# A fused attention and feed-forward kernel: the cast of x moved from ScalarE to GpSimd, and new orders on four engines

## The chip, the core and the metric
The kernel runs on one core of a Trainium2 chip. The metric is the device time of one execution in microseconds (us). The engines are TensorE (PE; its weight loads are PEld), VectorE (DVE), ScalarE (ACT), GpSimd (POOL) and SyncE (SP), which here only issues DMAs. Each engine runs its own list of instructions in order; semaphores tie the lists together.

## The reference
x has the shape (16, 128, 32, 32): 16 batches of 1024 tokens with 128 channels. What is computed, cut to what matters:

```
x  = einsum('oc,bchw->bohw', inv(I - circulant(ricker(width, damp))), x)
t  = tokens(x)                                  # (16, 1024, 128)
t1 = t + attention(layernorm(t))                # causal linear attention, 8 heads of 16,
                                                # features elu(.) + 1, running sums of K V and of K
z  = layernorm(t1)
g  = mean over tokens of (relu(z gfc1' + b) gfc2' + b)
W1m = W1 + sum_e g_e tv_W1[e]     W2m = W2 + sum_e g_e tv_W2[e]      # weights of each batch
out = t1 + layernorm(z + W2m relu(W1m z + b1m) + b2m) * gain + bias
```

## The kernel before
The first phase (some 20 to 490 us) goes over 128 tiles of 128 tokens, eight to a batch, and makes t1, z and the sums of the gate. The second phase is the feed-forward part. The diff touches only the first phase.

Nearly every product is made from float16 parts: a tensor is split into a high part (its float16 cast) and a low part (the rest, again cast), and three products are added. For x the parts are x_hi and x_lo, two tiles (128x256) to an instruction.

What sets the order is written out by hand. Each engine has a table such as SCALAR_ORDER: names of stages, each with a skew. In slot s the engine runs, for each name in the table's order, that stage for tile s - skew. One pass over the eight slots of a batch is `batch`; `run` unrolls the first two batches, loops over the middle ones and unrolls the rest. An engine whose next instruction waits on a semaphore holds up all that stands behind it.

The stages that the change and the prediction speak of:
- split_x stands in two tables. On ScalarE (L722) it makes x_hi; on GpSimd (L1036) it makes x_lo when x_hi is ready. Both act in even slots, for tiles s and s + 1. x_hi has room for eight tiles, so the cast waits (`wo_done`) until out_project has read the tiles eight back.
- conv (L559) and project (L571) multiply x by the inverse and by the weights of q, k and v. stats1 and mean_var1 take the layernorm's variance from conv's result, and rsqrt (L977, GpSimd) makes the factor, for both layernorms at once.
- exp_qk, relu_qk, v_hi (ScalarE), make_qk and v_lo (VectorE) form q, k and v. qk_hi and qk_lo (GpSimd) split q and k, and SyncE's turn (L467) transposes the parts by DMA (qkT_parts).
- scores (L606), scores_hi and scores_lo make the causal products in p_a; values (L629) multiplies by v and adds the state of earlier tiles; denominator, invert and divide finish the attention; turn_out, copy_out and out_project (L660) bring it back and add conv's product a second time, from the same x_hi and x_lo.
- read_t1, stats2, mean_var2, shift2, normalise, z_hi, z_lo (GpSimd) and SyncE's turn_z make z and its transposed parts; gate and gate_relu use them.
- tv_hi and tv_lo (L844, VectorE) split the expert weights, a quarter of a share of each batch at a time; they serve the second phase.

The lists of instructions are in PSUM's and SBUF's terms double or fourfold buffered: p_in has two banks, p_a one set, qkT_parts and z_parts four places.

Of the kernel before, what the change touches and what calls it, by code (L numbers as in the profile page):

```python
# [11 lines left out]
ACT = mybir.ActivationFunctionType  # L12
AX = mybir.AxisListType

B, C, T = 16, 128, 1024
P = 128
TILES = T // P
NT = B * TILES
HALF = 4
# [19 lines left out]

TENSOR_ORDER = [("state", 3), ("scores", 4), ("conv", 0), ("turn_out", 6), ("values", 5), ("out_project", 6),
                ("gate", 13), ("project", 0)]
SCALAR_ORDER = [("normalise", 10), ("split_x", 0), ("relu_qk", 2), ("read_t1", 7), ("gate_relu", 14),
                ("exp_qk", 1), ("state_hi", 3), ("v_hi", 1), ("tv_hi", 0), ("scores_hi_0", 4), ("copy_out", 6),
                ("scores_hi_1", 4)]
VECTOR_ORDER = [("shift2", 9), ("divide", 6), ("make_qk", 2), ("v_lo", 2), ("stats2", 7), ("stats1", 0),
                ("state_lo", 3), ("mean_var1", 0), ("mean_var2", 7), ("scores_lo_0", 4), ("denominator", 5),
                ("scores_lo_1", 4), ("tv_lo", 1), ("invert", 5)]
GPSIMD_ORDER = [("rsqrt", 1), ("z_hi", 10), ("split_x", 0), ("z_lo", 10), ("qk_hi", 2), ("qk_lo", 2),  # L50
                ("last_rsqrt2", 8)]
SYNC_ORDER = [("turn_z", 10), ("turn", 2), ("load_x", 3), ("load_tv", 3), ("store", 8)]

# [76 lines left out]
def build(nc, d):  # L130

    top = ExitStack()
    with top:
# [61 lines left out]
        x_loaded = [sem(f"x_loaded_{i}") for i in range(2)]  # L195
        ones_set = sem("ones_set")
# [12 lines left out]
        xh_ready, xl_ready = sem("xh_ready"), sem("xl_ready")  # L209
# [172 lines left out]
        with early, ExitStack() as pa_:  # L382
# [41 lines left out]
            def at_least(eng, s, value):  # L424

                if not isinstance(value, int) or value > 0:
                    eng.wait_ge(s, value)

            def batch(stages, b, behind=None):

                for slot in range(TILES):
                    for k, stage_ in stages:
                        d, t = divmod(slot - k, TILES)
                        if isinstance(b, int) and not 0 <= b + d < B:
                            continue
                        stage_(b + d, t)
                    if behind:
                        behind(TILES * (b - B) + slot)

            def run(eng, order, stages, behind=None):  # L440
                stages = [(skew, stages[name]) for name, skew in order]
                for b in range(2):
                    batch(stages, b)
                with eng.Fori(2, B) as b:
                    batch(stages, b)
                for b in range(B, B + 2):
                    batch(stages, b, behind)

            MEAN, VAR, RSTD, SHIFT = 9, 10, 11, 12
            PAIRED = 7  # L450
# [4 lines left out]
            with nc.Block() as block:  # L455
# [263 lines left out]

                @block.scalar  # L720
                def _(act):
                    def split_x(b, t):  # L722
                        if t % 2 or isinstance(b, int) and TILES * b + t == 0:
                            return
                        n = TILES * b + t
                        hf, j = t // HALF, t % HALF
                        if j == 0:
                            act.wait_ge(x_loaded[hf], 16 * (b + 1))
                        at_least(act, wo_done, n - TILES + 2)
                        cols = slice(j * P, (j + 2) * P)  # L730
                        nc.scalar.activation(xh[:, hf, cols], xf[:, hf, cols], ACT.Copy).then_inc(xh_ready, 1)

                    def tv_hi(b, t):
                        if t % 2:
                            return
# [79 lines left out]
                    def merged_w1_hi(slot):  # L815
# [6 lines left out]
                                             p_in[:, k % 2, :].rearrange("p (j m) -> p m j", j=4), ACT.Copy)\  # L822
                            .then_inc(mhi_ready, 1)

                    run(act, SCALAR_ORDER, {"tv_hi": tv_hi, "split_x": split_x, "read_t1": read_t1, "v_hi": v_hi,
                        "exp_qk": exp_qk, "relu_qk": relu_qk,
                        "scores_hi_0": scores_hi(0), "scores_hi_1": scores_hi(1),
                        "copy_out": copy_out, "normalise": normalise, "state_hi": state_hi, "gate_relu": gate_relu}, merged_w1_hi)
# [144 lines left out]
                @block.gpsimd  # L973
                def _(pool):
                    mhalf = kcol("mhalf")

                    def rsqrt(b, t):  # L977
                        n = TILES * b + t
                        both = not isinstance(n, int) or n >= PAIRED
                        pool.wait_ge(mv1, n + 1)  # L980
                        if both:
                            pool.wait_ge(mv2, n - PAIRED + 1)
                        s = sts[:, 0:2 if both else 1, t % 4, :]
                        nc.gpsimd.tensor_tensor(s[:, :, RSTD], s[:, :, VAR], mhalf[:, 0:2 if both else 1], ALU.pow)\  # L984
                            .then_inc(rstd, 1)

                    def last_rsqrt2(b, t):
                        n = TILES * b + t
                        if not isinstance(n, int) or n < NT - PAIRED:
                            return  # L990
                        s = st2[:, (t + 3) % 4, :]
                        pool.wait_ge(mv2, n + 1)
                        nc.gpsimd.tensor_tensor(s[:, RSTD:RSTD + 1], s[:, VAR:VAR + 1], mhalf[:, 0:1], ALU.pow)\
                            .then_inc(rstd, 1)

                    def parts_at(t, q_at, k_at, dims):

                        tile = pk[:, t % 4, :, :, :].rearrange("p w h c -> p (w h c)")
                        return bass.AP(tile.tensor, tile.offset + q_at,
                                       [list(tile.ap[0]), [NH * 4 * DH + k_at - q_at, 2], [4 * DH, NH], *dims])  # L1000

                    def qk_hi(b, t):
                        n = TILES * b + t
                        made, used = (n + 1, n - 3) if isinstance(n, int) else (pool.to_reg(n + 1), pool.to_reg(n - 3))
                        pool.wait_ge(ones_set, 1)
                        pool.wait_ge(qk_ready, made)
                        for i in range(2):
                            at_least(pool, sc_done[i], used)
                        src = qk[:, t % 4, :].rearrange("p (w h i) -> p w h i", h=NH, i=DH)
                        nc.gpsimd.tensor_copy(parts_at(t, 0, DH, [[DH, 2], [1, DH]]),  # L1010
                                              src.unsqueeze(3).broadcast_to([P, 2, NH, 2, DH])).then_inc(hi_ready, 1)

                    def qk_lo(b, t):
                        n = TILES * b + t
                        pool.wait_ge(hi_ready, n + 1)
                        nc.gpsimd.tensor_tensor(parts_at(t, 2 * DH, 0, [[1, DH]]),  # L1016
                                                qk[:, t % 4, :].rearrange("p (w h i) -> p w h i", h=NH, i=DH),
                                                pk[:, t % 4, :, :, DH:2 * DH], ALU.subtract).then_inc(lo_ready, 1)

                    def z_hi(b, t):  # L1020
                        n = TILES * b + t
                        made, used = n + 1, 32 * b + 16 * (t // 4)
                        if not isinstance(n, int):
                            made, used = pool.to_reg(made), pool.to_reg(used)
                        pool.wait_ge(ones_set, 1)
                        pool.wait_ge(z_ready, made)
                        at_least(pool, z_turned[t % 4], used)
                        nc.gpsimd.tensor_copy(zp[:, t % 4, 0, :], z_[:, t % 2, :]).then_inc(zhi_ready, 1)

                    def z_lo(b, t):  # L1030
                        n = TILES * b + t
                        pool.wait_ge(zhi_ready, n + 1)
                        nc.gpsimd.tensor_tensor(zp[:, t % 4, 1, :], z_[:, t % 2, :], zp[:, t % 4, 0, :], ALU.subtract)\
                            .then_inc(zlo_ready, 1)

                    def split_x(b, t):  # L1036
                        if t % 2 or isinstance(b, int) and TILES * b + t == 0:
                            return
                        hf, j = t // HALF, t % HALF
                        cols = slice(j * P, (j + 2) * P)  # L1040
                        pool.wait_ge(xh_ready, TILES // 2 * b + t // 2 + 1)
                        nc.gpsimd.tensor_tensor(xl[:, hf, cols], xf[:, hf, cols], xh[:, hf, cols], ALU.subtract)\
                            .then_inc(xl_ready, 1)

                    run(pool, GPSIMD_ORDER, {"rsqrt": rsqrt, "qk_lo": qk_lo,
                        "split_x": split_x,
                        "last_rsqrt2": last_rsqrt2, "qk_hi": qk_hi, "z_hi": z_hi, "z_lo": z_lo})


        with ExitStack() as pb:  # L1050
# [428 lines left out]
```

## Time and profile before

| | us |
|---|---|
| median of 3 runs | 747.9 (747.24 to 750.97) |
| profiled execution | 749.55 |
| its span, first to last instruction | 747.8 |

| engine | busy us | share of the span | instructions |
|---|---|---|---|
| PE | 692.5 | 93% | 12002 |
| PEld | 533.8 | 71% | 12002 |
| DVE | 659.1 | 88% | 2409 |
| ACT | 649.1 | 87% | 1780 |
| POOL | 465.2 | 62% | 790 |

The mean clock granted to TensorE is 0.975 of full speed. In the slices of the page PE, DVE and ACT stand at 90% or more through the steady part of the first phase, POOL at 80% or more; after about 470 us DVE, ACT and above all POOL have less to do. The time that SyncE takes to issue a DMA isn't counted as busy in this table; it is seen in the timeline of its queue (SPq). A duration is that of one instruction from its start to its end, and consecutive instructions of an engine may overlap by some tens of nanoseconds, so start to start is often less.

### The profile page before, as it was taken

The numbers are of one execution on the slowest core, as the hardware profiler recorded it, in microseconds if no ns is written. First come the engines' busy times: TensorE is split into PE (matmuls) and PEld (weight loads), VectorE is DVE, ScalarE is ACT, GpSimd is POOL, SyncE is SP. The second block draws the span as 40 slices with busy tenths as digits, with TensorE's granted clock in tenths as the row PEclk, the third lists the DMA queues.
The fourth block names the chain that finished last, engine by engine and source line by source line (L and its number), as shares of the span: only waits on it lengthen the run. The fifth ranks groups of instructions, "written<-read, shape, count | busy, mean of one in ns | idle before, by whom it ended". The sixth has DMA issues, their size and how long they took to land. (4 is left out here: it accounts for less than half of the span.)

```text
span 747.8 us, 38168 instructions
## 1 busy us (share of the span) xinstructions
PE 692.5 (93%) x12002; PEld 533.8 (71%) x12002; DVE 659.1 (88%) x2409; ACT 649.1 (87%) x1780; POOL 465.2 (62%) x790
## 2 busy tenths in 40 slices
PE   4898899999999999999999999888999998999993
PEld 2576677777777777777777777775777787777772
DVE  5697889999999999999999999768898977998983
ACT  4797989999999999999999999557888876888883
POOL 3686778888888888888888888421333321333333
PEclk9798999999999999999999999899999999999998
DMA  4757676666666666666666666410222211222221
GB/s 149 112 110 134 132 129 129 148 143 131 148 142 132 148 141 132 148 141 134 148 139 135 148 142 123 74 51 1 73 85 83 71 58 31 85 70 84 84 84 70
DMA packets 202485, 82.66 MB, mean 111 GB/s; under 512 B 176093, under 2 KB 189824, under 8 KB 202377
## 3 DMA queue, kind: packets, MB, share of 16 engines
q1 hardware_dynamic: 202440, 82.08, 48.3%
q8 instruction: 26, 0.43, 0.2%
q14 instruction: 19, 0.15, 0.1%
HBM read 22.79 MB, written 17.30 MB: 54 GB/s over the span
## 5 line engine op out<-in xcount | busy, mean ns | idle before, releaser
L892 DVE SCALAR_TENSOR_TENSOR scores_lo<-p_a,scores_hi 128x512 f16<-128x512 f32 x256 | 173.3, 683 | 1.7 <-ACT scores_hi L786 1.3
L786 ACT ACTIVATE scores_hi<-p_a 128x512 f16<-128x512 f32 x256 | 156.2, 611 | 9.3 <-PE p_a L623 9.3
L1010 POOL CAST qk_parts<-qk_f 128x512 f16<-128x512 f32 x128 | 78.0, 610 | 50.2 <-issue 24.9
L1442 POOL TENSOR_TENSOR ffn_rstd_shift<-ffn_rstd_shift,consts 128x4 f32<-128x4 f32 x32 | 36.5, 1142 | 109.1 <-DVE ffn_rstd_shift L1400 109.1
L984 POOL TENSOR_TENSOR stats<-stats,consts 128x2 f32<-128x2 f32 (+1 forms) x128 | 88.2, 689 | 17.9 <-DVE stats L925 13.1
L1224 PE MATMUL psb<-merged_W_of_batch,h_hi 128*128 128x128 f16 x512 | 94.5, 220 | 2.2 <-DVE h_lo L1378 1.5
L1378 DVE TENSOR_TENSOR h_lo<-h_f,h_hi 128x512 f16<-128x512 f32 x128 | 95.6, 786 | 1.1 <-ACT h_hi L1280 1.1
L1269 ACT ACTIVATE h_f<-psb,merged_b_of_batch 128x512 f32<-128x512 f32 x128 | 87.2, 709 | 10.3 <-PE psb L1205 8.6
L1225 PE MATMUL psb<-merged_W_of_batch,h_hi 128*128 128x128 f16 x512 | 94.2, 220 | 0.0
L1226 PE MATMUL psb<-merged_W_of_batch,h_lo 128*128 128x128 f16 x512 | 94.1, 220 | 0.0
L1016 POOL TENSOR_TENSOR qk_parts<-qk_f,qk_parts 128x256 f16<-128x256 f32 x128 | 85.9, 671 | 10.2
L640 PE MATMUL p_o<-v_parts,scores_hi 128*128 128x17 f16 x1024 | 90.3, 171 | 1.8 <-issue 0.2
L640 PEld LDWEIGHTS p_o<-v_parts,scores_hi 128*128 128x128 f16 x1024 | 82.1, 96 | 12.4 <-issue 11.7
L644 PE MATMUL p_o<-v_parts,scores_lo 128*128 128x17 f16 x1024 | 89.8, 171 | 0.0
L642 PE MATMUL p_o<-v_parts,scores_hi 128*128 128x16 f16 x1024 | 89.6, 170 | 0.0
L642 PEld LDWEIGHTS p_o<-v_parts,scores_hi 128*128 128x128 f16 x1024 | 80.5, 96 | 1.0
L644 PEld LDWEIGHTS p_o<-v_parts,scores_lo 128*128 128x128 f16 x1024 | 80.1, 96 | 0.0
L1435 POOL TENSOR_TENSOR normed<-normed,ln_gain_rows 128x512 f32<-128x512 f32 x32 | 40.6, 1268 | 59.5 <-ACT normed L1289 59.5
L1289 ACT ACTIVATE normed<-psb,ffn_rstd_shift 128x128 f32<-128x128 f32 x128 | 48.1, 456 | 33.8 <-DVE ffn_rstd_shift L1406 33.8
L801 ACT ACTIVATE z<-t,stats 128x128 f32<-128x128 f32 x128 | 65.5, 512 | 0.9 <-DVE stats L875 0.9
L765 ACT ACTIVATE exp_qk<-p_in,stats 128x256 f32<-128x256 f32 x128 | 60.8, 475 | 3.7 <-POOL stats L984 2.1
L616 PE MATMUL p_a<-mask_factors_bf 64*128 64x256 bf16 x512 | 60.2, 277 | 3.5 <-DVE scores_lo L892 1.2
(215 smaller groups left out, 2697.5 us busy)
## 6 DMA issues: line engine op xcount, KB each, us to landing
x_f<-in_x SPq DMA_DIRECT2D x32, 256.0 KB, 3.2
t_rows<-t SPq DMA_DIRECT2D x64, 128.0 KB, 1.8
t_back<-t_rows SPq DMA_DIRECT2D x32, 256.0 KB, 2.6
out<-out_tile SPq DMA_DIRECT2D x32, 256.0 KB, 2.1
tv_share<-in_L_ffn_tv_W SPq DMA_DIRECT2D x32, 128.0 KB, 2.2
qkT_parts<-qk_parts SPq DMA_TRANSPOSE x128, 3.1
zT_hi_lo<-z_parts SPq DMA_TRANSPOSE x128, 2.3
merged_W<-in_L_ffn_W SPq DMA_DIRECT2D x2, 256.0 KB, 4.4
```

The source lines that it names most:

```text
L640: mm(num[:, h, :], hi, vp[:, t, h, 0:VW], start=(h == 0), stop=False, skip_group_check=True)
L642: mm(num[:, h, 0:DH], hi, vp[:, t, h, VW:VW + DH], start=False, stop=False, skip_group_check=True)
L644: last = mm(num[:, h, :], lo, vp[:, t, h, 0:VW], start=False, stop=True, skip_group_check=True)
L786: nc.scalar.activation(ah[:, t % 2, cols], p_a[:, cols], ACT.Relu).then_inc(ahi_ready[eo], 1)
L892: nc.vector.scalar_tensor_tensor(al[:, t % 2, cols], p_a[:, cols], 0.0, ah[:, t % 2, cols], ALU.max, ALU.subtract).then_inc(alo_ready[eo], 1)
L984: nc.gpsimd.tensor_tensor(s[:, :, RSTD], s[:, :, VAR], mhalf[:, 0:2 if both else 1], ALU.pow)\
L1016: nc.gpsimd.tensor_tensor(parts_at(t, 2 * DH, 0, [[1, DH]]), qk[:, t % 4, :].rearrange("p (w h i) -> p w h i", h=NH, i=DH), pk[:, t % 4, : ...
L1224: mm(o, hi, w2b[:, bb, 0, c, :], start=False, stop=False)
L1225: mm(o, hi, w2b[:, bb, 1, c, :], start=False, stop=False)
L1226: last = mm(o, lo, w2b[:, bb, 0, c, :], start=False, stop=(c == FC - 1))
L1269: nc.scalar.activation(hf_[:, c, :], ps[:, c, :], ACT.Relu, bias=b1s[:, h // 2, c:c + 1], scale=1.0 / WS).then_inc(h_ready[c], 1)
L1378: nc.vector.tensor_tensor(hl[:, h % 2, c, :], hf_[:, c, :], hh[:, h % 2, c, :], ALU.subtract)\
```

## The change
ScalarE's split_x goes. GpSimd gets it as x_hi with skew -1: in odd slots, as the last stage, for the two tiles of the next slot; the old split_x of GpSimd is now x_lo and stands right behind rsqrt. tv_lo of VectorE moves from behind the scores_lo pair to behind mean_var1. Stages change places in the tables of TensorE, ScalarE and VectorE; SYNC_ORDER stays. GpSimd's loop ends one batch earlier (`upto`), since the last batch has no next tiles to cast.

```diff
-TENSOR_ORDER = [("state", 3), ("scores", 4), ("conv", 0), ("turn_out", 6), ("values", 5), ("out_project", 6),
-                ("gate", 13), ("project", 0)]
+TENSOR_ORDER = [("state", 3), ("scores", 4), ("turn_out", 6), ("conv", 0), ("values", 5), ("gate", 13),
+                ("out_project", 6), ("project", 0)]
...
-GPSIMD_ORDER = [("rsqrt", 1), ("z_hi", 10), ("split_x", 0), ("z_lo", 10), ("qk_hi", 2), ("qk_lo", 2),
+GPSIMD_ORDER = [("rsqrt", 1), ("x_lo", 0), ("z_hi", 10), ("z_lo", 10), ("qk_hi", 2), ("qk_lo", 2), ("x_hi", -1),
...
-            def run(eng, order, stages, behind=None):
+            def run(eng, order, stages, behind=None, upto=B):
...
-                with eng.Fori(2, B) as b:
+                with eng.Fori(2, upto) as b:
                     batch(stages, b)
-                for b in range(B, B + 2):
-                    batch(stages, b, behind)
+                for b in range(upto, B + 2):
+                    batch(stages, b, behind if b >= B else None)
...
-                    def split_x(b, t):
-                        if t % 2 or isinstance(b, int) and TILES * b + t == 0:
-                            return
-                        n = TILES * b + t
-                        hf, j = t // HALF, t % HALF
-                        if j == 0:
-                            act.wait_ge(x_loaded[hf], 16 * (b + 1))
-                        at_least(act, wo_done, n - TILES + 2)
-                        cols = slice(j * P, (j + 2) * P)
-                        nc.scalar.activation(xh[:, hf, cols], xf[:, hf, cols], ACT.Copy).then_inc(xh_ready, 1)
...
+                    def x_hi(b, t):
+                        if t % 2 or isinstance(b, int) and TILES * b + t == 0:
+                            return
+                        n = TILES * b + t
+                        hf, j = t // HALF, t % HALF
+                        loaded, used = 16 * (b + 1), n - TILES + 2
+                        if not isinstance(n, int):
+                            loaded, used = pool.to_reg(loaded), pool.to_reg(used)
+                        pool.wait_ge(ones_set, 1)
+                        if j == 0:
+                            pool.wait_ge(x_loaded[hf], loaded)
+                        at_least(pool, wo_done, used)
+                        cols = slice(j * P, (j + 2) * P)
+                        nc.gpsimd.tensor_copy(xh[:, hf, cols], xf[:, hf, cols]).then_inc(xh_ready, 1)
+
+                    def x_lo(b, t):
```

On GpSimd, at the border of an odd slot and the even one behind it, in the loop, the list was this. qk_f, qk_parts are q and k and their parts, stats holds the factors of rsqrt, x_f, x_hi and x_lo are x and its parts, z_parts those of z:

```order
L1004 REGISTER_ALU
L1010 CAST qk_parts<-qk_f 128x2x8x32 [waits sc_done_0,sc_done_1,qk_ready,ones_set]
L1016 TENSOR_TENSOR qk_parts<-qk_f,qk_parts 128x2x8x16 [waits hi_ready]
L980 REGISTER_ALU
L982 REGISTER_ALU [waits mv1]
L984 TENSOR_TENSOR stats<-stats,consts 128x2 [waits mv2]
L1024 REGISTER_ALU
L1028 CAST z_parts<-z 128x128 [waits z_turned_0,z_ready,ones_set]
L1041 REGISTER_ALU
L1042 TENSOR_TENSOR x_lo<-x_f,x_hi 128x256 [waits xh_ready]
```

Now, with the code's lines a little earlier, the same place reads:

```order
L998 CAST qk_parts<-qk_f 128x2x8x32 [waits sc_done_0,sc_done_1,qk_ready,ones_set]
L1004 TENSOR_TENSOR qk_parts<-qk_f,qk_parts 128x2x8x16 [waits hi_ready]
L1031 ISA
L1037 CAST x_hi<-x_f 128x256 [waits wo_done,ones_set]
L968 REGISTER_ALU
L970 REGISTER_ALU [waits mv1]
L972 TENSOR_TENSOR stats<-stats,consts 128x2 [waits mv2]
L1044 REGISTER_ALU
L1045 TENSOR_TENSOR x_lo<-x_f,x_hi 128x256 [waits xh_ready]
L1012 REGISTER_ALU
```

The cast x_hi has come in between qk_lo and rsqrt, with its wait on out_project (wo_done), and x_lo has moved up from behind z_hi to behind rsqrt.

On VectorE, in an odd slot of the loop, from the two variances (BN_AGGR; the one that waits on bn1 is mean_var1, on bn2 mean_var2) to invert (RECIPROCAL), the list was this:

```order
L842 BN_AGGR stats<-stats 128x2 [waits bn1,ones_set]
L925 BN_AGGR stats<-stats 128x2 [waits bn2,ones_set]
L890 REGISTER_ALU [waits av_done]
L892 SCALAR_TENSOR_TENSOR scores_lo<-p_a,scores_hi 128x512 [waits ahi_ready_0]
L899 TENSOR_SCALAR denominators<-p_o 128x8 [waits av_done]
L892 SCALAR_TENSOR_TENSOR scores_lo<-p_a,scores_hi 128x512 [waits ahi_ready_1,av_done]
L848 ISA
L850 ISA [waits tv_hi_ready]
L850 SCALAR_TENSOR_TENSOR tv_lo<-tv_share,tv_hi 128x128
L905 RECIPROCAL denominators<-denominators 128x8 [waits den1]
```

Now, from state_lo (state_parts) on:

```order
L871 TENSOR_TENSOR state_parts<-p_s,state_parts 128x136 [waits sh_ready]
L830 BN_AGGR stats<-stats 128x2 [waits bn1,ones_set]
L836 ISA
L838 ISA [waits tv_hi_ready]
L838 SCALAR_TENSOR_TENSOR tv_lo<-tv_share,tv_hi 128x128
L878 REGISTER_ALU [waits av_done]
L880 SCALAR_TENSOR_TENSOR scores_lo<-p_a,scores_hi 128x512 [waits ahi_ready_0]
L887 TENSOR_SCALAR denominators<-p_o 128x8 [waits av_done]
L880 SCALAR_TENSOR_TENSOR scores_lo<-p_a,scores_hi 128x512 [waits ahi_ready_1,av_done]
L893 RECIPROCAL denominators<-denominators 128x8 [waits den1]
```

tv_lo stood between the second scores_lo and invert; now it stands between mean_var1 and the first scores_lo, and mean_var2 has gone further ahead.

## Rows read from the trace of the kernel before

**Rows 1.** Busy time of each engine, 130 to 450 us: window, its length, then PE, PEld, DVE, ACT, POOL
```profile
130.00:450.00 320.00, 307.54 (x6468) 237.42 (x6468) 309.46 (x1228) 317.42 (x999) 270.84 (x505) 1.00 0.65 141
```

**Rows 2.** Waits of SyncE's queue, 73 to 456 us: total us, times, longest us
```profile
SPq L427 <- POOL qk_parts L1016: 1.3, 4, 0.7
```

**Rows 3.** Timeline of SyncE's queue, one batch: start us, duration us, instruction
```profile
297.36 1.23 SPq L473 DMA_TRANSPOSE qkT_parts<-qk_parts  x1
...
300.37 1.18 SPq L482 DMA_TRANSPOSE zT_hi_lo<-z_parts  x1
...
303.94 1.17 SPq L482 DMA_TRANSPOSE zT_hi_lo<-z_parts  x1
305.31 1.23 SPq L473 DMA_TRANSPOSE qkT_parts<-qk_parts  x1
...
308.83 1.23 SPq L473 DMA_TRANSPOSE qkT_parts<-qk_parts  x1
...
325.33 1.23 SPq L473 DMA_TRANSPOSE qkT_parts<-qk_parts  x1
```

**Rows 4.** The tile qk_parts, 130 to 450 us: ns min/median/max, and landing
```profile
L473 SPq DMA_TRANSPOSE qkT_parts<-qk_parts x92: 1231/1232/1382, 129.3 to 448.2; - x92
...
DMA to landing us min/median/max: 3.0/3.1/3.3
```

**Rows 5.** Timeline of GpSimd around the even slot of tile 82
```profile
303.99 0.70 POOL L984 TENSOR_TENSOR stats<-stats,consts 128x2 f32<-128x2 f32 x1
304.64 0.29 POOL L1028 CAST z_parts<-z 128x128 f16<-128x128 f32 x1
304.89 0.79 POOL L1042 TENSOR_TENSOR x_lo<-x_f,x_hi 128x256 f16<-128x256 f32 x1
...
306.04 0.61 POOL L1010 CAST qk_parts<-qk_f 128x512 f16<-128x512 f32 x1
306.73 0.68 POOL L1016 TENSOR_TENSOR qk_parts<-qk_f,qk_parts 128x256 f16<-128x256 f32 x1
...
309.83 0.67 POOL L1016 TENSOR_TENSOR qk_parts<-qk_f,qk_parts 128x256 f16<-128x256 f32 x1
```

**Rows 6.** Timeline of ScalarE (first row) and TensorE, same stretch
```profile
304.33 0.42 ACT L731 ACTIVATE x_hi<-x_f 128x256 f16<-128x256 f32 x1
...
303.86 0.44 PE L669 MATMUL p_m<-w_outT,attn_outT 128*128 128x128 f32 x2
...
305.91 0.23 PE L567 MATMUL p_m<-w_in_hi,x_hi 128*128 128x128 f16 x1 [0.22 <-POOL x_lo L1042]
...
306.09 0.28 PE L658 MATMUL p_m<-consts,attn_out 128*128 128x128 f32 x1
306.38 0.17 PE L640 MATMUL p_o<-v_parts,scores_hi 128*128 128x17 f16 x1
...
310.70 0.44 PE L669 MATMUL p_m<-w_outT,attn_outT 128*128 128x128 f32 x2
...
312.15 0.39 PE L623 MATMUL p_a<-qkT_parts 64*128 64x128 f16 x8
```

**Rows 7.** Timeline of VectorE (L850, L842) and GpSimd (L1042), two slots
```profile
304.87 0.28 DVE L850 SCALAR_TENSOR_TENSOR tv_lo<-tv_share,tv_hi 128x128 f32 x1
...
310.23 0.18 DVE L842 BATCH_NORM_AGGREGATE stats<-stats 128x2 f32<-128x9 f32 x1
...
318.59 0.67 POOL L1042 TENSOR_TENSOR x_lo<-x_f,x_hi 128x256 f16<-128x256 f32 x1
318.73 0.67 DVE L850 SCALAR_TENSOR_TENSOR tv_lo<-tv_share,tv_hi 128x128 f32 x1
```

**Rows 8.** Waits of SyncE's queue, 20 to 73 us, then 456 to 500 us
```profile
SPq L427 <- POOL qk_parts L1016: 9.2, 5, 3.1
SPq L471 <- POOL qk_parts L1016: 4.1, 4, 2.8
...
SPq L481 <- POOL z_parts L1033: 8.7, 6, 2.4
```

More of the change, by code:

```diff
@@ L38 @@
 BIG = -1.0e30
-TENSOR_ORDER = [("state", 3), ("scores", 4), ("conv", 0), ("turn_out", 6), ("values", 5), ("out_project", 6),
-                ("gate", 13), ("project", 0)]
[L44 to L49, printed above, removed]
-GPSIMD_ORDER = [("rsqrt", 1), ("z_hi", 10), ("split_x", 0), ("z_lo", 10), ("qk_hi", 2), ("qk_lo", 2),
+TENSOR_ORDER = [("state", 3), ("scores", 4), ("turn_out", 6), ("conv", 0), ("values", 5), ("gate", 13),
+                ("out_project", 6), ("project", 0)]
+SCALAR_ORDER = [("relu_qk", 2), ("normalise", 10), ("read_t1", 7), ("gate_relu", 14), ("state_hi", 3),
+                ("tv_hi", 0), ("exp_qk", 1), ("v_hi", 1), ("copy_out", 6), ("scores_hi_0", 4), ("scores_hi_1", 4)]
+VECTOR_ORDER = [("shift2", 9), ("divide", 6), ("stats2", 7), ("make_qk", 2), ("mean_var2", 7), ("v_lo", 2),
+                ("stats1", 0), ("state_lo", 3), ("mean_var1", 0), ("tv_lo", 1), ("scores_lo_0", 4),
+                ("denominator", 5), ("scores_lo_1", 4), ("invert", 5)]
+GPSIMD_ORDER = [("rsqrt", 1), ("x_lo", 0), ("z_hi", 10), ("z_lo", 10), ("qk_hi", 2), ("qk_lo", 2), ("x_hi", -1),
                 ("last_rsqrt2", 8)]
@@ L823, in merged_w1_hi @@
                             .then_inc(mhi_ready, 1)
-                    run(act, SCALAR_ORDER, {"tv_hi": tv_hi, "split_x": split_x, "read_t1": read_t1, "v_hi": v_hi,
+                    run(act, SCALAR_ORDER, {"tv_hi": tv_hi, "read_t1": read_t1, "v_hi": v_hi,
                         "exp_qk": exp_qk, "relu_qk": relu_qk,
@@ L1034, in z_lo @@
                             .then_inc(zlo_ready, 1)
-                    def split_x(b, t):
+                    def x_hi(b, t):
[13 more added lines that the diff above has]
+                    def x_lo(b, t):
                         if t % 2 or isinstance(b, int) and TILES * b + t == 0:
@@ L1045, in _ @@
                     run(pool, GPSIMD_ORDER, {"rsqrt": rsqrt, "qk_lo": qk_lo,
-                        "split_x": split_x,
-                        "last_rsqrt2": last_rsqrt2, "qk_hi": qk_hi, "z_hi": z_hi, "z_lo": z_lo})
+                        "x_hi": x_hi, "x_lo": x_lo,
+                        "last_rsqrt2": last_rsqrt2, "qk_hi": qk_hi, "z_hi": z_hi, "z_lo": z_lo}, upto=B - 1)
         with ExitStack() as pb:
```

## The prediction, made before the result was known

> **What bounds the kernel now.** I read the busy shares first, then the waits, then the order of time of one queue. In the long steady stretch of the first phase ScalarE is busy for 317 of 320 us, VectorE for 309 and TensorE for 308 [rows 1], so ScalarE looks like the bound, and the change takes work from it. The waits say otherwise. The queue that issues the DMAs (SyncE) waits 1.3 us in all between 73 and 456 us, four times [rows 2]: of 383 us it stands idle for a third of a per cent. Its timeline is one issue behind another, 1.2 us for each transpose, two transposes a tile [rows 3, 4]. From the transpose of q and k at 297.36 to the same one a batch later at 325.33 it takes 27.97 us for eight tiles [rows 3]. The queue is late, not early: the parts of tile 80 are finished at 306.73 + 0.68 = 307.41 [rows 5], their transpose is issued at 308.83 [rows 3], lands 3.1 us later [rows 4] at about 311.93, and TensorE takes it up at 312.15 [rows 6]. So finished work waits for the queue, and the reader of the result comes just behind the landing. Neither side has time to give away.
>
> A second cycle is as long. A pair of tiles of x can be cast only when out_project has read the pair whose place it takes. In [rows 6] out_project ends at 303.86 + 0.44 = 304.30 (call this O). The cast starts on ScalarE at 304.33 and takes 0.42, x_lo on GpSimd runs from 304.89 to 305.68 [rows 5], and conv starts at 305.91, after an idle 0.22 that ends with x_lo [rows 6]. O to conv is 1.61. From conv to the end of out_project two slots on (310.70 + 0.44 = 311.14) TensorE takes 5.23. Together that is 6.84 for this pair of tiles, against 27.97 / 4 = 6.99 for the queue. Four such pairs make a batch, and the other pairs are as near. So the steady stretch, 383 / 27.97 = 13.7 batches, has two bounds of nearly one length.
>
> **The change part by part.**
> SyncE: its program is unchanged, instruction for instruction, so 27.97 us a batch is a floor that the change does not touch. Nothing gained elsewhere shortens the steady stretch.
>
> ScalarE: 63 casts of 0.42 go. They lie beside the queue's floor; worth 0.
>
> GpSimd: 63 casts of 128x256 come. No such cast stands in the trace. The casts beside it are z_hi with 128 columns, 0.29, and qk_hi with 512, 0.61 [rows 5]; these are my bounds, and the straight line between them gives 0.40. GpSimd is busy for 271 of 320 us [rows 1]; 46 casts of 0.40 are 18.4, which makes 289, or 90%: it fits, but with little room.
>
> The wait for out_project moves with the cast. On ScalarE it was the second stage of the even slot; now it stands last in the odd slot of GpSimd, and behind it are queued rsqrt, then x_lo. That the cast is a slot ahead in the program doesn't make it earlier: out_project of the pair seven tiles back ends at O in either case. The new path from O to conv: the wake, 0.14 (as from the cast's end at 304.75 to x_lo at 304.89; below, the 0.03 of ScalarE); the cast, 0.40 (0.29 to 0.61); rsqrt, 0.65 from start to start, 303.99 to 304.64 (0.70 by its duration) [rows 5]; x_lo, 0.67 undisturbed [rows 7] (0.79 in [rows 5]); conv, 0.23 as now. The sum is 2.09, between 1.85 and 2.47, where it was 1.61.
>
> TensorE: turn_out goes ahead of conv. It held up the products with v by 0.29 (306.09 to 306.38) [rows 6]; ahead of conv it falls into time in which conv waits for x_lo. Conv to O is then 5.23 - 0.29 = 4.94. The gate's change of place with out_project adds nothing: both lie between the same conv and the same later out_project.
>
> VectorE: tv_lo leaves its place ahead of invert. It takes 0.28 when it starts before x_lo, and 0.67 when x_lo is 0.14 ahead [rows 7]; then invert, divide and turn_out come late. I take the pair without this delay (the 5.23 above) for all four, so this gain is in the sum. In its new place tv_lo stands ahead of both scores_lo. On GpSimd qk_lo runs from 309.83 to 310.50 [rows 5] where mean_var1 ends at 310.41 [rows 7], so it will still meet an operation there and may be held by 0.67 - 0.28 = 0.39. Behind it wait scores_lo and then the next scores on TensorE. That stretch of TensorE has the 0.22 in which it idles now, plus 2.09 - 1.61 = 0.48, less 0.29 for turn_out, or 0.41. The hold is just covered: 0, and if the cover goes 0.1 a pair costs 5.5 us in all (4 x 13.7 pairs).
>
> The Trainium skill, SBUF — State Buffer (Who interferes with whom), says that a VectorE instruction with two inputs in SBUF and a GpSimd instruction that reads SBUF exclude each other, and that the one that starts first holds the other up. The trace agrees: 0.28 or 0.67 by which of the two was first. By that rule the new place, too, costs a hold in each pair; what that would make is the third rival.
>
> ScalarE's other stages and the rest of VectorE's order change their places beside the floor; with no row that shows a wait of theirs, 0. The stretches outside the floor, where SyncE waits for its data (9.2 and 4.1 us before 73 us, 8.7 after 456 [rows 8]), may move either way: 0, with 5 us on both sides.
>
> Sum: a pair takes 2.09 + 4.94 = 7.03, a batch 28.12, 0.15 over the queue's 27.97; 13.7 batches make +2.1 us. The profiled execution took 749.55 (its span 747.8 and 1.75 around it), so it would take 751.6; the median shown is 1.65 lower, and the forecast is **750.0**. Not a gain, because the queue's floor stays, and hardly a loss, because the new chain is about as long as the floor.
>
> **The rivals.**
> First, GpSimd's chain decides and the kernel is slower. It decides from 27.97 / 4 - 4.94 = 2.05 us between O and conv; each 0.1 above is 5.5 us. With the cast at 0.51, half way to the row of 512 columns, the chain is 2.20, and the time 747.9 + 0.15 x 54.8 = 756; at 2.47 it is 771. For it: every step is in one queue behind one wait, and the forecast lies only 0.04 above the point. Against it: the row nearest to the cast in kind is z_hi, the shorter one.
>
> Second, the steady stretch stays, and its ends get shorter: ScalarE loses 0.42 in each pair and tv_lo its 0.39 in some; in some six pairs of the first batches and of the last that is up to 5 us, 743. For it: SyncE waits there for GpSimd's parts. Against it: GpSimd gets the cast there too.
>
> Third, the hold on tv_lo isn't covered. At 0.2 a pair it costs 0.2 x 54.8 = 11, so 759. For it: qk_lo and mean_var1 end within 0.1 us of each other. Against it: the spare 0.41 on TensorE. It decides as soon as the hold is over 0.41.
>
> Fourth, ScalarE really is the bound: 63 x 0.42 = 26 us would go, 722. Against it speaks the queue without waits; I see no way around that.
>
> **How the numbers follow.** Forecast 0.48, first rival 0.32, second 0.09, third 0.08, fourth 0.03. Half a per cent, 3.7 us, is about what can be told from no change. Faster by more: second and fourth, 0.12. Slower by more: first and third, 0.40. Same: 0.48. The forecast's own range is 746 to 752. The range for 8 in 10 leaves out the fourth rival, a part of the second, and the upper end of the first and third: 744.5 to 759.5.
>
> **What would show it.** In the changed profile: SyncE again almost without waits between 73 and 456 us, and a batch of 27.97 there, if the floor holds; if a batch is longer, waits of SyncE for qk_parts appear. ScalarE's busy share falls by about 6% and shows idle time. x_hi on GpSimd starts 0.1 to 0.2 behind the end of out_project and takes 0.40; rsqrt starts at once behind it; conv of every even slot waits for x_lo, some 2.1 behind O. No invert waits behind a long tv_lo. The forecast is wrong if SyncE's batch gets shorter than 27.9 us (its issues then weren't a floor), or if x_hi starts well before O or runs for over 0.5.

## The result, and the profile after

The changed kernel takes 762.57 us (median of 4 runs, 760.76 to 764.65), the kernel before 748.91 on the same chip (747.24 to 750.97): a ratio of 1.018, with a 95% interval of 1.015 to 1.021. It is slower by 13.7 us; the forecast was 750.0, with a range up to 759.5. The profiled execution has a span of 759.0 us against 747.8.

The loss lies in the steady stretch of the first phase. The view of one tile gives a measure of a batch that works for every kernel here: x_lo runs four times a batch, and the row gives its number and its first and last start between 130 and 450 us. Before, then after (nanoseconds min/median/max, first to last start in us):

```profile
L1042 POOL TENSOR_TENSOR x_lo<-x_f,x_hi x46: 668/722/795, 130.1 to 444.5; 128x256 f16<-128x256 f32 x46
```
```profile
L1045 POOL TENSOR_TENSOR x_lo<-x_f,x_hi x45: 669/672/677, 130.3 to 448.0; 128x256 f16<-128x256 f32 x45
```
(444.5 - 130.1) / 45 x 4 is 27.95 us a batch before; (448.0 - 130.3) / 44 x 4 is 28.88 after. The 0.93 times 13.7 batches is 12.7 us: the whole loss, within the spread of single runs (13.7 by the medians, 11.2 by the two profiled spans). All batches given below are worked out in this way.

Busy time of the engines after, 130 to 450 us, answers to [rows 1], and the waits of SyncE's queue, 73 to 456 us, to [rows 2]:

```profile
130.00:450.00 320.00, 304.48 (x6246) 234.62 (x6247) 294.76 (x1189) 301.05 (x920) 275.14 (x533) 1.00 0.63 137
```
```profile
SPq L480 <- POOL z_parts L1021: 11.4, 46, 0.5
```
ScalarE went from 317 to 301 us, and no engine is as busy as before: this is a kernel that waits. SyncE, which had waited 1.3 us in all, waits 11.4 us for z_parts, so its queue is a bound no longer. Who waits instead is in the waits of the engines, same stretch (us in total, times, longest):

```profile
POOL x_hi L1037 <- PE p_m L668: 22.8, 44, 0.6
DVE stats L823 <- PE p_m L568: 19.9, 66, 0.5
PE p_a L615 <- DVE scores_lo L880: 11.0, 34, 0.4
```
Every one of the 44 casts on GpSimd waits for out_project. One circle of it, first on GpSimd, then on TensorE:

```profile
309.90 0.40 POOL L1037 CAST x_hi<-x_f 128x256 f16<-128x256 f32 x1 [0.59 <-PE p_m L668]
310.25 0.70 POOL L972 TENSOR_TENSOR stats<-stats,consts 128x2 f32<-128x2 f32 x1
310.92 0.68 POOL L1045 TENSOR_TENSOR x_lo<-x_f,x_hi 128x256 f16<-128x256 f32 x1
...
317.13 0.40 POOL L1037 CAST x_hi<-x_f 128x256 f16<-128x256 f32 x1 [0.62 <-PE p_m L668]
```
```profile
309.32 0.44 PE L668 MATMUL p_m<-w_outT,attn_outT 128*128 128x128 f32 x2
...
311.43 0.33 PE L657 MATMUL p_m<-consts,attn_out 128*128 128x128 f32 x1
311.83 0.23 PE L566 MATMUL p_m<-w_in_hi,x_hi 128*128 128x128 f16 x1
...
312.17 0.17 PE L639 MATMUL p_o<-v_parts,scores_hi 128*128 128x17 f16 x1
...
315.22 0.33 PE L657 MATMUL p_m<-consts,attn_out 128*128 128x128 f32 x1
315.39 0.22 PE L566 MATMUL p_m<-w_in_hi,x_hi 128*128 128x128 f16 x1
...
315.56 0.17 PE L639 MATMUL p_o<-v_parts,scores_hi 128*128 128x17 f16 x1
...
316.53 0.44 PE L668 MATMUL p_m<-w_outT,attn_outT 128*128 128x128 f32 x2
```
O, the end of out_project, is 309.32 + 0.44 = 309.76. The cast starts 0.14 behind it, rsqrt 0.35 behind the cast, x_lo 0.67 behind rsqrt, conv 0.91 behind x_lo: O to conv is 2.07. The next O is 316.97, 5.14 behind conv. Together 7.21, and the next cast starts 7.23 behind the first one: here the circle is closed. Conv starts 0.23 behind the end of x_lo (311.60), as it did in the kernel before, where its wait for x_lo was seen (305.68 to 305.91). The four pairs from this O on take 7.21, 7.12, 7.12 and 7.44, which makes 28.89. In the third of them the circle is hardly longer than TensorE's own row: conv starts 0.20 behind x_lo, but also only 0.16 behind turn_out, as in an odd slot, and TensorE had waited 0.28 for scores_lo just before.

### The profile page after: what moved, and what is told of

Read it like the earlier page. It is cut to its first block and busy times, and to the rows that moved or that the text cites. A ratio compares the mean times of both kernels' runs of the same rounds, so it can differ in the third digit from the quotient of the medians.

```text
span 759.0 us, 38200 instructions
## 1 busy us (share of the span) xinstructions
PE 698.3 (92%) x12002; PEld 538.8 (71%) x12002; DVE 653.6 (86%) x2409; ACT 638.3 (84%) x1717; POOL 484.5 (64%) x853
## 5 line engine op out<-in xcount | busy, mean ns | idle before, releaser
L774 ACT ACTIVATE scores_hi<-p_a 128x512 f16<-128x512 f32 x256 | 138.9, 601 | 0.7 <-PE p_a L622 0.7
L615 PE MATMUL p_a<-mask_factors_bf 64*128 64x256 bf16 x512 | 67.9, 277 | 17.0 <-DVE scores_lo L880 15.8
L823 DVE BATCH_NORM_STATS2 stats<-p_m 128x6 f32<-128x128 f32 x128 | 38.3, 299 | 37.8 <-PE p_m L568 36.4
```

Source lines behind the costliest of these rows:

```text
L774: nc.scalar.activation(ah[:, t % 2, cols], p_a[:, cols], ACT.Relu).then_inc(ahi_ready[eo], 1)
```

## The experiments

Each is timed beside the kernel before; "batch" is worked out from its x_lo row. Of the tables and functions the diffs show only the part that changes.

| kernel | median us | ratio to before (95%) | batch us |
|---|---|---|---|
| changed | 762.6 | 1.018 (1.015 to 1.021) | 28.88 |
| e1 changed, cast's wait open | 756.6 | 1.011 (1.009 to 1.013) | 28.52 |
| e2 changed, cast behind rsqrt | 757.2 | 1.012 (1.010 to 1.014) | 28.51 |
| e3 changed, tv_lo back | 762.2 | 1.019 (1.016 to 1.021) | 28.96 |
| e4 before + moved cast | 775.5 | 1.038 (1.034 to 1.042) | 30.13 |
| e5 before + new orders | 758.4 | 1.016 (1.012 to 1.019) | 28.60 |
| e17 before + tv_lo ahead | 748.7 | 1.000 (0.998 to 1.002) | 27.98 |
| e18 before + turn_out ahead | 772.6 | 1.031 (1.027 to 1.035) | 29.75 |
| e7 e2, tv_lo back | 782.2 | 1.050 (1.045 to 1.055) | 30.15 |
| e11 e2, turn_out back | 762.8 | 1.022 (1.018 to 1.026) | 28.99 |
| e12 e2, both back | 767.6 | 1.024 (1.019 to 1.028) | 29.34 |
| e6 before, cast's wait open | 748.2 | 1.000 (0.998 to 1.003) | 27.94 |
| e13 e12, loads on ScalarE | 765.3 | 1.021 (1.017 to 1.025) | 29.10 |
| e19 before, cast on GpSimd behind rsqrt | 746.8 | 0.999 (0.997 to 1.001) | 27.88 |
| e20 e19, tv_lo ahead | 748.4 | 1.000 (0.999 to 1.002) | 27.98 |
| e23 e19, ScalarE's new order | 766.4 | 1.022 (1.019 to 1.026) | 29.21 |
| e24 e19, gate ahead | 745.9 | 0.994 (0.992 to 0.996) | 27.94 |
| e21 before, tv_lo ahead, loads on ScalarE | 740.2 | 0.990 (0.986 to 0.993) | 27.48 |
| e22 e20, loads on ScalarE | 742.5 | 0.993 (0.991 to 0.995) | 27.59 |

**Is the circle through the cast the bound? (e1 to e4)**

e1 cuts it: out_project reads a constant tile (so its result leaves out x; one of its three such products is shown), and the cast waits only for the projection.

```diff
-mm(o, xh[:, hf, cols], wh[:, 0:C], start=True, stop=False)
+mm(o, xc[:, 0, :], wh[:, 0:C], start=True, stop=False)
...
-at_least(pool, wo_done, used)
+at_least(pool, in_done, used)
```


> The changed kernel, but out_project multiplies a constant tile in place of x's parts (same instructions, part of the result left out), so that the cast on GpSimd waits for project of the tiles eight back, long done, and no longer for out_project. Chain theory (out_project, x_hi, rsqrt, x_lo, conv in a circle set the 28.9 us of a batch): the circle is open, a batch falls to SyncE's 27.97 or little above, 748 to 751 us. VectorE theory (tv_lo ahead of scores_lo, and turn_out ahead of conv, make the slots late): stays at 758 to 763. Load theory (GpSimd has too much to do): stays at 758 to 763.

e2 keeps the wait and moves the cast behind rsqrt, into its own slot.

```diff
-GPSIMD_ORDER = [("rsqrt", 1), ("x_lo", 0), ... ("qk_lo", 2), ("x_hi", -1),
+GPSIMD_ORDER = [("rsqrt", 1), ("x_hi", 0), ("x_lo", 0), ... ("qk_lo", 2),
```


> The changed kernel with one stage moved: x_hi on GpSimd behind rsqrt, in the slot of its tiles, right ahead of x_lo, where rsqrt no longer stands behind its wait. Work and waits are the same. Chain theory: out_project to conv falls from 2.1 by rsqrt's 0.66 to about 1.45, a batch to SyncE's 27.97, 748 to 751 us. VectorE theory: 758 to 763. Load theory: 758 to 763.

e3 puts only tv_lo back to its old place.

```diff
-("mean_var1", 0), ("tv_lo", 1), ("scores_lo_0", 4), ("denominator", 5), ("scores_lo_1", 4), ("invert", 5)
+("mean_var1", 0), ("scores_lo_0", 4), ("denominator", 5), ("scores_lo_1", 4), ("tv_lo", 1), ("invert", 5)
```


> The changed kernel with tv_lo of VectorE back behind the second scores_lo. Chain theory: nothing that counts, 760 to 765 us (tv_lo may meet x_lo again). VectorE theory: the 0.3 to 0.5 us ahead of scores_lo go, 4 times a batch, 748 to 755.

e4 is the other half: the kernel before with the cast and x_lo moved on GpSimd as in the change, and none of the other orders.

```diff
-SCALAR_ORDER = [("normalise", 10), ("split_x", 0), ("relu_qk", 2), ...
+SCALAR_ORDER = [("normalise", 10), ("relu_qk", 2), ...
-GPSIMD_ORDER = [("rsqrt", 1), ("z_hi", 10), ("split_x", 0), ("z_lo", 10), ("qk_hi", 2), ("qk_lo", 2),
+GPSIMD_ORDER = [("rsqrt", 1), ("x_lo", 0), ("z_hi", 10), ("z_lo", 10), ("qk_hi", 2), ("qk_lo", 2), ("x_hi", -1),
```


> The kernel before with only the cast moved: x_hi on GpSimd a slot ahead, x_lo behind rsqrt, ScalarE without the cast; TensorE's, VectorE's and ScalarE's other orders as before. Chain theory: the circle is there and turn_out stands behind conv again, which adds up to 0.1 a pair: 760 to 770 us. VectorE theory: the loss comes from the new orders, so 748 to 754.

Opening the circle in either way takes 5 to 6 us off the changed kernel, and e3 nothing. So the circle is its bound at 28.9, but only just: 28.5 is the next one, by e1 and e2 alike, and neither comes down to the 748 to 751 us that the chain theory gave. e4, at 775.5, is above its forecast too, and in it the same wait is the greatest of all, 1 us at a time:

```profile
POOL x_hi L1038 <- PE p_m L669: 42.1, 43, 2.3
```
In the old orders the moved cast costs 27 us, so the new orders earn half of that back; and yet something in them holds the batch at 28.5 when the cast doesn't.

**What do the new orders cost alone? (e5, e17, e18)**

e5 leaves the cast on ScalarE and takes the new tables of TensorE, VectorE and ScalarE (as in the diff of the change, with split_x behind normalise).

> The kernel before, with the cast on ScalarE, but with the new orders of TensorE, VectorE and ScalarE. Theory (two circles: the one through the cast on GpSimd makes 28.9 of the changed kernel, the one through the new orders 28.5): with the cast on ScalarE the first is 4 x (1.61 + 5.10) = 26.8 and out of the way, the second is left: 28.5 a batch, 755 to 758 us. Rival (the orders cost nothing, all of the loss is the cast's): 27.97 a batch, 747 to 750 us.

```profile
L849 DVE SCALAR_TENSOR_TENSOR tv_lo<-tv_share,tv_hi 128x128 f32 x44 | 16.2, 369 | 1.5
```
(behind the bars: busy us in all and mean ns of one, then idle time before them.) 10 us come without any moved cast. With the cast on ScalarE (e5), on GpSimd without its wait (e1) or behind rsqrt (e2), the new orders make 28.5 to 28.6. By itself e5 doesn't show that this is a bound without the cast: on ScalarE the cast stands behind normalise, and in the pair whose out_project ends at 307.94 it starts only at 308.44, x_lo ends at 309.64 and conv starts 0.24 behind that, as where it waits for x_lo. In e2 conv starts 0.45 to 0.62 behind x_lo, so there it waits for something else. The next two take one edit of the new orders each.

```diff
-("mean_var2", 7), ("scores_lo_0", 4), ("denominator", 5), ("scores_lo_1", 4), ("tv_lo", 1), ("invert", 5)
+("mean_var2", 7), ("tv_lo", 1), ("scores_lo_0", 4), ("denominator", 5), ("scores_lo_1", 4), ("invert", 5)
```


> The kernel before, cast on ScalarE, with one edit: tv_lo ahead of the first scores_lo. Theory (the spare of 0.41 on TensorE covers tv_lo while turn_out stands behind conv): 747 to 751 us. Rival (tv_lo ahead of scores_lo costs by itself, since TensorE's scores wait for scores_lo): 754 to 760 us, with TensorE waiting for scores_lo 0.3 to 0.4 at a time.

```diff
-("conv", 0), ("turn_out", 6), ("values", 5)
+("turn_out", 6), ("conv", 0), ("values", 5)
```


> The kernel before, cast on ScalarE, with one edit: turn_out ahead of conv on TensorE. Theory (turn_out waits for divide, which stands behind tv_lo and invert; conv, ahead of it before, waits with it now): 755 us or more, with TensorE waiting for divide ahead of conv. Rival (divide is there in time when the cast doesn't lie beside tv_lo): 747 to 751 us.

tv_lo ahead costs nothing. Its group of rows in e17, then in e18:

```profile
L850 DVE SCALAR_TENSOR_TENSOR tv_lo<-tv_share,tv_hi 128x128 f32 x45 | 14.1, 313 | 1.8
```
```profile
L850 DVE SCALAR_TENSOR_TENSOR tv_lo<-tv_share,tv_hi 128x128 f32 x43 | 29.6, 689 | 0.0
```
turn_out ahead costs 24 us, with the cast still on ScalarE. The waits of e18, 130 to 450 us, and its timeline over 2 us on GpSimd, VectorE and TensorE (put together from three answers, each in its order):

```profile
PE p_m L658 <- DVE attn_out L911: 17.9, 43, 0.5
...
PEld p_m L658 <- DVE attn_out L911: 11.9, 22, 0.6
```
```profile
308.65 0.67 POOL L1042 TENSOR_TENSOR x_lo<-x_f,x_hi 128x256 f16<-128x256 f32 x1
```
```profile
308.79 0.68 DVE L850 SCALAR_TENSOR_TENSOR tv_lo<-tv_share,tv_hi 128x128 f32 x1
309.39 0.19 DVE L905 RECIPROCAL denominators<-denominators 128x8 f32<-128x8 f32 x1
...
309.70 0.29 DVE L911 TENSOR_TENSOR attn_out<-p_o,denominators 128x128 f32<-128x128 f32 x1
...
310.85 0.30 DVE L835 BATCH_NORM_STATS2 stats<-p_m 128x6 f32<-128x128 f32 x1
```
```profile
310.12 0.32 PE L658 MATMUL p_m<-consts,attn_out 128*128 128x128 f32 x1 [0.51 <-DVE attn_out L911]
310.47 0.23 PE L567 MATMUL p_m<-w_in_hi,x_hi 128*128 128x128 f16 x1
```
Read it as a chain: x_lo on GpSimd starts first and tv_lo beside it takes 0.68 in place of 0.28; invert and divide stand behind it; turn_out waits 0.51 for divide, conv stands behind turn_out, and the first variance (stats) behind conv. VectorE then does scores_lo behind that variance, and tv_lo and divide again behind scores_lo. That is a second circle, without the cast, between TensorE and VectorE. Before, conv stood ahead of turn_out and had no part in it. tv_lo has one: it is 0.32 shorter in e5 than in e18 (0.369 against 0.689), four a batch make 1.28, and the batches differ by 1.15. e5 has the other new orders as well, so this alone doesn't show that the difference is tv_lo's; e7 beside e2, below, differ in tv_lo's place alone, by 25 us. In the new orders the two edits belong together: tv_lo ahead takes back most of what turn_out ahead costs, but not all.

The Trainium skill, SBUF — State Buffer (Who interferes with whom), names the pair: a VectorE instruction with two inputs in SBUF and a GpSimd one that reads SBUF exclude each other. By that rule tv_lo beside x_lo is held, and the trace agrees: 0.68 against 0.28 [rows 7]. Not every GpSimd instruction beside tv_lo holds it: in e3 it lies beside rsqrt (128x2, from 310.72 to 311.42; tv_lo from 310.97 to 311.25) and takes 0.28 at the mean.

```profile
L838 DVE SCALAR_TENSOR_TENSOR tv_lo<-tv_share,tv_hi 128x128 f32 x44 | 12.3, 280 | 0.0
```
So tv_lo's old place brings no hold in e3: there GpSimd waits for out_project first, and x_lo comes later than tv_lo.

**A square of four, and one table more (e2, e7, e11, e12, e23, e24)**

From e2, one edit is put back (e7, e11) or both (e12): tv_lo as in the diff of e3, turn_out by the reverse of the diff of e18.

> x_hi stands behind rsqrt, so that the circle through out_project's cast is open, and tv_lo goes back behind the second scores_lo. Theory (a second circle, through VectorE's scores_lo, holds the new orders at 28.5 us a batch, and tv_lo is 0.41 of each pair in it): the batch loses up to 4 x 0.41 = 1.6 and meets the floor of SyncE's issue queue, 27.97; 748 to 751 us, and SyncE hardly waits between its transposes. Rival (the circle runs on through invert, shift2, divide and turn_out, in which tv_lo stands in either place): the batch stays at 28.4 to 28.6, 755 to 758 us. Second rival (SyncE's queue, which now waits, was never a floor): below 745 us.

> x_hi stands behind rsqrt as in the kernel before it, and turn_out goes back behind conv on TensorE. Theory (turn_out ahead of conv closes the second circle: conv of a slot waits for VectorE's divide): the circle is cut at conv, and the batch meets the floor of 27.97; 748 to 751 us. Rival (the second circle runs through scores_lo, values, gate and out_project alone, whatever the place of turn_out): the batch stays at 28.4 to 28.6, 755 to 758 us.

> x_hi behind rsqrt, and both tv_lo (behind the second scores_lo) and turn_out (behind conv) back in their old places: with the two kernels that put back one each and the one that puts back neither, this fills a square of four (757.2 with neither, 782.2 with tv_lo, 762.8 with turn_out). Theory (the loss of the new orders lies in a circle through VectorE that each half closes in its own way: tv_lo behind scores_lo holds divide, on which turn_out and with it conv waits; tv_lo ahead holds scores_lo): with both back the batch meets SyncE's floor of 27.97, 747 to 752 us. Rival (the cast on GpSimd itself, which then keeps VectorE from its rows, costs the rest): 756 us or more, and not below the kernel with neither.

The theory failed in all three. e12's time is in its rival's range, but that rival's cause, the cast on GpSimd, is answered by e19 below, where the cast is free. e7 is the worst of all: turn_out ahead with tv_lo behind scores_lo is e18 again, with tv_lo held.

```profile
L838 DVE SCALAR_TENSOR_TENSOR tv_lo<-tv_share,tv_hi 128x128 f32 x43 | 28.2, 656 | 0.0
```
e11 and e12 have turn_out behind conv, and yet 28.99 and 29.34. So a third part of the new orders costs. From e19 (below: old orders, cast on GpSimd behind rsqrt, 746.8) one table each:

```diff
-("normalise", 10), ("relu_qk", 2), ... ("exp_qk", 1), ("state_hi", 3), ("v_hi", 1), ("tv_hi", 0), ("scores_hi_0", 4), ("copy_out", 6), ("scores_hi_1", 4)
+("relu_qk", 2), ("normalise", 10), ... ("state_hi", 3), ("tv_hi", 0), ("exp_qk", 1), ("v_hi", 1), ("copy_out", 6), ("scores_hi_0", 4), ("scores_hi_1", 4)
```


> Old orders, cast on GpSimd behind rsqrt (746.8), with the new order of ScalarE alone, in which copy_out stands ahead of both scores_hi. Theory (copy_out waits for turn_out, which behind conv comes later, and both scores_hi wait behind it; in the kernel with the rest of the new orders VectorE waits 0.3 for scores_hi at 46 places): 757 to 770 us, with that wait. Rival (ScalarE's order is free): 746 to 751 us.

```diff
-("values", 5), ("out_project", 6), ("gate", 13), ("project", 0)
+("values", 5), ("gate", 13), ("out_project", 6), ("project", 0)
```


> Old orders, cast on GpSimd behind rsqrt (746.8), with gate ahead of out_project on TensorE alone. Theory (ScalarE's order is the costly part): 746 to 752 us. Rival (out_project is later by the gate's products in each second slot, and the circle through it is longer): 754 us or more.

The gate's place is free: its batch is the floor's 27.94. ScalarE's order costs 17 to 20 us while turn_out stands behind conv. ScalarE in e23, its waits between 130 and 450 us, and one of them in the timeline:

```profile
ACT attn_outT L766 <- PE p_m L657: 25.8, 44, 0.7
```
```profile
307.53 0.28 ACT L766 ACTIVATE attn_outT<-p_m 128x128 f32<-128x128 f32 x1 [0.53 <-PE p_m L657]
307.70 1.08 ACT L774 ACTIVATE scores_hi<-p_a 128x512 f16<-128x512 f32 x2
```
copy_out stands ahead of both scores_hi and waits 0.53 for turn_out; both scores_hi stand behind it. The same wait is 25.8 us in e11 and 24.0 in e12, which have this table and turn_out behind conv. The table moves other stages too; that copy_out's place is what costs is read from this wait and not tested alone. So turn_out has to be early for ScalarE's order, and then VectorE's divide has to be early for TensorE: each table needs the others, and all of them together still make 28.5.

What is waited for at 28.5 is seen in e2, where TensorE no longer waits for divide. The waits of e2 between 130 and 450 us, then one circle on VectorE and on TensorE:

```profile
PE p_a L615 <- DVE scores_lo L880: 15.2, 45, 0.4
DVE stats L823 <- PE p_m L568: 11.4, 45, 0.4
```
```profile
306.13 0.30 DVE L823 BATCH_NORM_STATS2 stats<-p_m 128x6 f32<-128x128 f32 x1 [0.40 <-PE p_m L568]
...
306.77 0.29 DVE L838 SCALAR_TENSOR_TENSOR tv_lo<-tv_share,tv_hi 128x128 f32 x1
...
307.66 0.68 DVE L880 SCALAR_TENSOR_TENSOR scores_lo<-p_a,scores_hi 128x512 f16<-128x512 f32 x1
```
```profile
308.48 0.38 PE L615 MATMUL p_a<-mask_factors_bf 64*128 64x256 bf16 x3 [0.40 <-DVE scores_lo L880]
...
309.18 0.22 PE L566 MATMUL p_m<-w_in_hi,x_hi 128*128 128x128 f16 x1
```
VectorE's first variance waits for conv, tv_lo and both scores_lo follow, TensorE's scores wait for scores_lo, and turn_out and the next conv stand behind scores. Each wait comes once a pair. So here the circle runs through scores_lo and not through divide; no run opens it alone.

**Is SyncE's queue the floor, and what lies below it? (e6, e19, e20, e13, e21, e22)**

e6 is the kernel before with the edit of e1 (its cast on ScalarE).

> The kernel before, with the circle through the cast cut: out_project multiplies a constant tile in place of x_hi and x_lo (its numbers are left out of the result; its instructions are as many), and ScalarE's cast waits for the projection alone. Theory (the issue queue of SyncE is the floor of the kernel before, 27.97 a batch): no gain, 746 to 749 us, and SyncE hardly waits. Rival (the circle of 6.84 a pair, or the waits of TensorE in it, holds the kernel before): 4 to 10 us faster, 738 to 744 us.

No gain, 27.94 a batch: in the kernel before the circle through the cast was not what held it. SyncE's waits in e6, 73 to 456 us:

```profile
SPq L429 <- POOL qk_parts L1018: 1.4, 3, 0.7
SPq L483 <- POOL z_parts L1035: 0.2, 1, 0.2
```
e19 and e20 take the old orders with the cast on GpSimd behind rsqrt (the diff of e2 on e4); e20 adds the edit of e17.

> The orders of the kernel before, the cast on GpSimd behind rsqrt, where out_project is long over, with x_lo behind it. Theory (the price of the moved cast in the old orders, 27 us, is its place a slot ahead, where it waits for out_project and holds rsqrt): 748 to 755 us, and no wait of x_hi for out_project. Rival (the cast costs on GpSimd wherever it stands, since rsqrt, cast and x_lo in one row end only 1.8 us behind the start of rsqrt and conv waits for x_lo): 760 us or more, with TensorE waiting for x_lo.

> The kernel beside it with tv_lo ahead of the first scores_lo. Theory (tv_lo ahead of scores_lo is free in the old orders, and is shorter there if x_lo doesn't lie beside it): the same as the kernel beside it within 3 us. Rival (with cast and x_lo in one row on GpSimd tv_lo ahead lies beside x_lo and holds scores_lo): 4 us or more slower.

In e19 the cast is free. On GpSimd it stands between rsqrt and x_lo, with no wait:

```profile
302.92 0.70 POOL L973 TENSOR_TENSOR stats<-stats,consts 128x2 f32<-128x2 f32 x1
303.61 0.40 POOL L1038 CAST x_hi<-x_f 128x256 f16<-128x256 f32 x1
304.08 0.77 POOL L1046 TENSOR_TENSOR x_lo<-x_f,x_hi 128x256 f16<-128x256 f32 x1
```
So neither GpSimd's 0.40 nor its load is the cost; the place a slot ahead, in which the cast waits and rsqrt behind it, is. The last three take two of SyncE's DMAs a batch away from it.

```diff
-SYNC_ORDER = [("turn_z", 10), ("turn", 2), ("load_x", 3), ("load_tv", 3), ("store", 8)]
+SYNC_ORDER = [("turn_z", 10), ("turn", 2), ("load_x", 3), ("store", 8)]
...
-("v_hi", 1), ("tv_hi", 0),
+("v_hi", 1), ("load_tv", 3), ("tv_hi", 0),
```


> The kernel beside it (x_hi behind rsqrt, tv_lo and turn_out back), and the two loads of tv_share of each batch are issued by ScalarE, which the cast has left, in place of SyncE. Theory (SyncE's queue of issues is the floor there): it loses 2 x 0.39 = 0.78 a batch, 27.2, up to 10 us: 738 to 745 us. Rival (another engine or wait holds that kernel too): no gain over the kernel beside it.

> The kernel before with tv_lo ahead of scores_lo (which alone moved nothing, 748.7) and the two loads of tv_share of each batch issued by ScalarE in place of SyncE. Theory (SyncE's issue queue, 27.97 a batch, hides what the rest could do): it falls to 27.2, and the circle of 6.84 a pair, 27.4, or ScalarE with 27.7 busy a batch, is next: 740 to 746 us. Rival (ScalarE, busy for 316.8 of 320 us, is as much a floor as SyncE): 748 us or more.

> The second kernel of this job with the two loads of tv_share issued by ScalarE, which there has no cast to do. If the second kernel stands at SyncE's floor (747 to 750), this one falls below it, 738 to 746 us; if it stands above the floor by a wait, this one stands where it stands.

e13, on e12 with its waits, gains nothing that can be told; e21 and e22, on kernels at the floor, fall below it, e21 to 740.2 us, the fastest kernel here and faster than both. Its waits of SyncE, 73 to 456 us, and its busy times, 130 to 450 us:

```profile
SPq L427 <- POOL qk_parts L1018: 9.3, 32, 0.5
SPq L481 <- POOL z_parts L1035: 2.8, 12, 0.6
```
```profile
130.00:450.00 320.00, 308.05 (x6577) 242.66 (x6574) 309.00 (x1248) 318.96 (x1015) 274.04 (x514) 1.00 0.67 143
```
Now SyncE waits, and ScalarE is busy for 319 of 320 us: by that it is most likely the next floor, which no run tests. What holds e22 at 27.59, where ScalarE is busy for 307, was not taken apart.

## Why the prediction was wrong

**SyncE's queue as a floor of 27.97: right.** e6, e17, e19, e20 and e24 stand on it, 27.88 to 27.98, whatever was opened above it; in the last four SyncE's queue has no wait at all between 73 and 456 us; and e21 and e22 go below it when issues leave the queue. The fourth rival (ScalarE is the bound) was wrong of the kernel before; in e21 it may come true.

**O to conv, 2.09: right.** 2.07 here; the cast takes 0.40 as taken from the two rows beside it. In one pair of four it is 2.28: there rsqrt starts 0.55 behind the cast's start (302.49 to 303.04), in place of 0.35. That this is the border of the loop over batches is likely and not shown.

**Conv to O, 5.23 - 0.29 = 4.94: the step that failed.** It is 5.14, and 5.10 at the mean of the four pairs (5.14, 5.03, 5.09, 5.15). I took the whole 0.29 of turn_out off because it would lie in the wait for x_lo. Before, the products with v followed conv by 306.38 - 305.91 = 0.47 in the even slot [rows 6], and in the odd one by 0.29 with turn_out between:

```profile
309.44 0.23 PE L567 MATMUL p_m<-w_in_hi,x_hi 128*128 128x128 f16 x1
...
309.61 0.28 PE L658 MATMUL p_m<-consts,attn_out 128*128 128x128 f32 x1
309.73 0.17 PE L640 MATMUL p_o<-v_parts,scores_hi 128*128 128x17 f16 x1
```
After, the even slot has 312.17 - 311.83 = 0.34, which is 0.13 less and not 0.29, and the odd slot 315.56 - 315.22 = 0.34 from turn_out on, 0.05 more. In a row of TensorE's turn_out costs its time from start to start, 0.12 in the odd slot before (309.61 to 309.73) and 0.17 after (315.22 to 315.39), and not its duration of 0.28 to 0.33; that is a larger overlap than the tens of nanoseconds I had written of. The other 0.17 of the 0.29 wasn't turn_out's: after the change the products with v still start 0.34 behind conv in the even slot and 0.17 in the odd one (315.39 to 315.56). What delays them there isn't shown; it isn't conv's wait alone, since in the third pair, with no idle time ahead of conv, it is 0.29 (326.12 to 326.41). The 0.20 lost in this way moves the point from which GpSimd's chain decides from 2.05 to 6.99 - 5.14 = 1.85, and the chain of 2.07 to 2.28 lies well above it. So the mechanism is the first rival's (chance 0.32, 756 to 771 us), reached by the other term; that 762.6 lies in that rival's range is partly luck, since what it let grow, the cast, came out as forecast.

**The orders at 0: wrong, and the larger part.** I let turn_out's place count as a gain alone and ScalarE's and VectorE's orders as nothing, "with no row that shows a wait of theirs". turn_out ahead of conv makes conv wait for whatever divide waits for: 24 us alone (e18). ScalarE's order makes scores_hi wait for turn_out: 20 us alone (e23). In one kernel they help each other, and 8 to 10 us remain (e1, e2, e5), a bound of 28.5 to 28.6. The moves of stats2 and mean_var2 on VectorE were not run alone. The circle through the cast then adds 4 to 6 us (762.6 against 756.6, 757.2 and 758.4). These are not two prices to be added: the longer circle decides, and at 28.9 the cast's would hold the kernel by itself; opening it gives back only the distance to the next one.

**tv_lo's hold just covered: right for the place, by itself** (e17, no change), and in the changed kernel not the bound (e3, no change). The third rival fell in the form I gave it; tv_lo does count in the circle that turn_out ahead of conv closes.

**The signs.** Of those given ahead, SyncE waited for parts, x_hi started 0.14 behind O, as said, and ScalarE's busy time fell by 5%, where 6% was said. SyncE waited for z_parts and not for qk_parts. Neither of the two signs of being wrong came: the batch got longer than 27.9, not shorter, and the cast started behind O and took 0.40.

## What to carry to other kernels

When an instruction moves ahead of another in an in-order row, list what it waits for: everything behind it now waits for that too, and the price is that wait, not its duration. Cost each table of a set of orders alone, then together, since three that cost 0, 24 and 20 us alone may make 10 together. A cast that moves to an engine with time to spare is free only where it doesn't wait ahead of others in its row (27 us in e4, none in e19); and a gain above a floor is worth nothing until the floor is lowered, here by two DMA issues a batch.

## What the runs showed that I had not expected

Two loads a batch moved from SyncE to ScalarE shorten a batch by 0.50 us (27.98 in e17, 27.48 in e21), while ScalarE, full as it was, went only from 316.8 to 319.0 us of 320. Issuing isn't counted as busy; in e21 one load's issue takes 0.37 from 307.22 on, and an instruction of ScalarE starts at 307.31 beside it. x_lo with the same shape takes 0.67 in some kernels and 0.72 at the median in others, and in e19 at least 0.72 each time, without any change of GpSimd's own instruction.
